# A new written order for every step of a post-norm attention and LoRA-expert block, with the pieces of x used as they land and the last two tiles normalised by VectorE

## The chip, the cores and the metric

The kernel runs on one core of one Trainium2 chip. The metric is the device time of one launch in microseconds (us). Three timed runs of the kernel before gave 686.65, 687.94 and 688.41 us, median 687.94. A difference of about 0.3% (2.06 us) is what a measurement of this kernel can tell from no change.

## The reference

All inputs are float32. `x` is (2, 512, 512): 1024 rows of width 512.

```python
q = (x @ Wq).reshape(B, S, 32, 128)          # 32 query heads of 128
k = (x @ Wk).reshape(B, S, 8, 128)           # 8 key/value heads
v = (x @ Wv).reshape(B, S, 8, 128)
scores = einsum(q, repeat(k, 4)) * 128 ** -0.5, causal mask
out = softmax(scores) @ repeat(v, 4)
x = layernorm(x + out @ Wo)                  # eps 1e-5, no scale or bias
base = x @ W_base.T + b_base
weights = sparsemax(x @ W_router.T + b_router)      # 8 experts
h = x @ lora_A                                      # 8 experts, rank 16
x = layernorm(x + base + (h * weights) @ lora_B)
```

## The kernel before

**Tiles.** A unit u (16 of them) is one key/value head g with its four query heads for one batch entry b: u = 2 g + b. It has four tiles of 128 query rows over the four heads, t = 4 u + i, 64 in all. Tile t attends to 128 (i + 1) keys and is scored in four pieces `("S", t, h)` whose width grows from 32 (i = 0, h = 0) to 512 (i = 3, h = 3) columns in steps of 32.

**Two halves of each number.** Nearly every operand is held as a high and a low float16 half, so that one product is three matmuls (high by high, high by low, low by high). ScalarE writes the high half, VectorE or GpSimd the low one. All operands are first scaled by a power of two that is derived from the largest absolute value: `("most", ...)` is the maximum on VectorE, `("bits", stage)` the exponent, `("turn", stage)` a matmul on TensorE that carries the row maxima across partitions, `("factor", stage)` the scale on VectorE. Until the first scales exist, K(0) and Q(0, 0..3) are computed from the raw float32 pieces of x and of the weights (the list `FIRST`), which is line 1062 (K) and line 1082 (Q).

**The steps of one tile.** `S` on TensorE (line 1113); the masked minimum on VectorE as the score leaves PSUM (line 937); `exp` on ScalarE (781); `inv`, the reciprocal of the sums, on VectorE (945); `norm`, the high half of the probabilities, on ScalarE (790), with zeros written by GpSimd (691); `rest`, the low half on VectorE (957) and then a DMA that transposes the probabilities (SyncE's queue, line 627), two for each tile, q = 0 and 1; `PV` on TensorE (1128); `O_hi` and `O_lo`, the two halves of the product (797, 963); `W`, the output projection (1138); and its sum with x on VectorE (974).

**What sets the order.** Each engine runs its instructions in the order of one written list of steps: `FIRST_STEPS` up to tile 5, `NEXT_STEPS` for 16 tiles, run three times with shifted numbers (tiles 6 to 53), and `LAST_STEPS`. Every engine walks over the same list and issues the part that is its own, so that the list sets the order on all five engines and on SyncE's DMA queue. The steps that empty a PSUM bank are put in by `evicted`. Three banks rotate among S, turn, zt, R and ht, five among the others; a step takes the bank that was given back first in the list.

**The second half of the block.** For each of eight row tiles k: `st1`, `ln1` (statistics and first layer norm), `zt` (transpose on TensorE), `R` (router and LoRA A in one product), `sp` (the sparsemax, seven short instructions on VectorE after one copy of half the product by ScalarE, line 809), `base` (line 1170), `ht` (transpose of the weighted h, 1187), `F` (LoRA B, 1193), `st2` (statistics from PSUM on VectorE, 1035 and 1037; variance, power and, for tiles that ScalarE normalises, the product `nmr` on GpSimd, 706, 708 and 712), and `fin` (the second layer norm: ScalarE, line 820, for tiles 0 to 6; VectorE, line 1029, for tile 7), with its output DMA.

**Loads.** The first loads go over two queues: ScalarE issues x(0, 1), x(0, 3), wq(0, 1) and wq(0, 3), and SyncE all others, wk(0), x(0, 0), x(0, 2), wq(0, 0), wq(0, 2) first.

## Time and profile before

| | us |
|---|---|
| timed runs | 686.65, 687.94, 688.41 |
| median | 687.94 |
| the profiled execution, its own time | 687.11 |
| its span, first to last instruction | 685.3 |
| TensorE busy | 664.1 |
| VectorE busy | 540.3 |
| ScalarE busy | 413.8 |
| GpSimd busy | 278.9 |
| mean granted TensorE clock | 0.993 of full |

The span is the time from the first to the last instruction; the profiled execution's own time is 1.8 us longer. PE is TensorE's matmuls, PEld its weight loads, DVE VectorE, ACT ScalarE, POOL GpSimd, and SPq, ACTq and POOLq the sequencers that issue DMAs and wait. TensorE is busy for all but 21 us of the span, so what matters in this profile is where those 21 us lie and what ended each gap.

### The profile page before, as it was taken

Reading aid. Unit: us, or ns where it says so; the run is one execution under the profiler, and the core shown is the slowest. Engines: PE = TensorE matmul, PEld = TensorE weight load, DVE = VectorE, ACT = ScalarE, POOL = GpSimd, SP = SyncE. Lnnn points to the kernel's source line nnn. Section 1 sums busy time; section 2 is a strip of 40 time slices with the busy share of each in tenths; the row PEclk is TensorE's granted clock in tenths of the full one; section 3 lists DMA queues with packets and bytes.
Section 4 is the critical chain, followed back from the end, with each engine's and each line's share of the span. In section 5 each row is a group of like instructions: output and inputs, shape, how many; then the busy total and the mean of one; then the engine's idle time right before and its main releaser. Section 6 shows DMA issues by size and latency. Waiting matters only on the chain.

```text
span 685.3 us, 11621 instructions
## 1 busy us (share of the span) xinstructions
PE 664.1 (97%) x3606; PEld 355.5 (52%) x3606; DVE 540.3 (79%) x1704; ACT 413.8 (60%) x1072; POOL 278.9 (41%) x424
## 2 busy tenths in 40 slices
PE   6799999999999999999999999999999999999996
PEld 3365545445555555455554555454555545456675
DVE  4898879876897679876897679877887676799774
ACT  1667666666647665667557665667556664776232
POOL 1676962157105562158005661258005550152132
PEclk9899999999999999999999999999999999999999
DMA  9456367352924257343924277343824335464311
GB/s 291 126 134 160 60 118 170 64 90 55 238 54 93 48 122 170 63 86 74 230 48 88 46 133 161 63 84 79 204 46 82 58 67 109 89 128 78 77 48 61
DMA packets 200782, 71.82 MB, mean 105 GB/s; under 512 B 169744, under 2 KB 192784, under 8 KB 200720
## 3 DMA queue, kind: packets, MB, share of 16 engines
q1 hardware_dynamic: 199376, 70.04, 47.3%
q10 hardware_dynamic: 1344, 1.05, 0.6%
q8 instruction: 28, 0.46, 0.3%
q14 instruction: 34, 0.28, 0.1%
HBM read 27.02 MB, written 2.10 MB: 42 GB/s over the span
## 4 chain that ended last, share of the span: by engine, by line
PE 75%; POOL 7%; DMA 7%; DVE 5%; SPq 2%; ACT 2%; issue 2%; POOLq 0%; DVEq 0%; ACTq 0%
PE bank L1138 19%; PE bank L1089 16%; PE bank L1128 12%; PE bank L1113 10%; DMA pT<-p 6%; PE bank L1101 5%; POOL raw L678 3%; PE bank L1170 3%; PE bank L1069 3%; PE bank L1082 2%; DVE p L957 2%; SPq L627 2%; POOL wo_odd L681 2%; PE bank L1072 2%; PE bank L1181 1%
## 5 line engine op out<-in xcount | busy, mean ns | idle before, releaser
L678 POOL TENSOR_SCALAR raw<-raw,scale_of 128x512 f32<-128x512 f32 x76 | 120.2, 1581 | 161.9 <-ACT wk L740 65.4
L781 ACT ACTIVATE pr<-pr,mx 128x96 f32<-128x96 f32 (+15 forms) x256 | 131.4, 513 | 81.7 <-DVE mx L937 81.5
L957 DVE SCALAR_TENSOR_TENSOR p<-pr,ri,p 128x256 f16<-128x256 f32 (+15 forms) x256 | 137.2, 580 | 36.3 <-ACT p L790 36.2
L1089 PE MATMUL bank<-xT,wq 128*128 128x512 f16 x720 | 164.4, 379 | 0.0
L790 ACT ACTIVATE p<-pr,ri 128x32 f16<-128x32 f32 (+15 forms) x256 | 118.6, 512 | 72.2 <-DVE ri L948 54.9
L937 DVE CUSTOM_DVE_ANT_0 pr<-bank,mask,back_of 128x32 f32<-128x32 f32 (+15 forms) x256 | 124.0, 493 | 47.1 <-PE bank L1113 46.9
L1113 PE MATMUL bank<-kT,qT 128*128 128x32 f16 (+15 forms) x768 | 125.7, 281 | 4.3 <-DVE qT L843 1.9
L1128 PE MATMUL bank<-pT,v 128*128 128x512 f16 x480 | 123.3, 379 | 3.5 <-DMA pT<-p 3.3
L1089 PEld LDWEIGHTS bank<-xT,wq 128*128 128x128 f16 x720 | 70.5, 98 | 81.7
L1113 PEld LDWEIGHTS bank<-kT,qT 128*128 128x128 f16 x768 | 67.6, 98 | 64.1 <-issue 3.5
L691 POOL MEMSET p<- 128x64 f16 (+2 forms) x192 | 34.0, 204 | 163.3 <-DMA pT<-p 163.3
L1138 PE MATMUL bank<-wo_odd,oT 128*128 128x512 f16 x384 | 97.7, 379 | 0.0
L1138 PE MATMUL bank<-wo_even,oT 128*128 128x512 f16 x384 | 95.7, 379 | 0.2 <-DVE oT L963 0.2
L1128 PEld LDWEIGHTS bank<-pT,v 128*128 128x128 f16 x480 | 45.2, 98 | 48.8 <-issue 6.7
L1138 PEld LDWEIGHTS bank<-wo_even,oT 128*128 128x128 f16 x384 | 36.1, 98 | 35.3 <-issue 0.4
L1138 PEld LDWEIGHTS bank<-wo_odd,oT 128*128 128x128 f16 x384 | 36.0, 98 | 34.4 <-issue 1.2
L963 DVE SCALAR_TENSOR_TENSOR oT<-bank,oT 128x512 f16<-128x512 f32 x64 | 43.8, 685 | 12.6 <-ACT oT L797 12.6
L797 ACT ACTIVATE oT<-bank 128x512 f16<-128x512 f32 x64 | 37.5, 585 | 26.1 <-PE bank L1138 14.5
L1101 PE MATMUL bank<-wv,xT 128*128 128x256 f16 x384 | 48.4, 277 | 1.4 <-DVE wv L833 1.4
L781 ACT ACTIVATION_READ_ACCUMULATOR pr<-pr,mx 128x1 f32 x256 | 48.1, 188 | 0.0
L974 DVE SCALAR_TENSOR_TENSOR y<-bank,back_of,y 128x512 f32<-128x512 f32 x64 | 47.2, 742 | 0.6 <-PE bank L1138 0.6
L863 DVE TENSOR_REDUCE rowmax<-raw 128x1 f32<-128x2048 f32 (+2 forms) x28 | 46.7, 1669 | 0.7 <-DMA raw<-in_wq 0.7
(121 smaller groups left out, 731.3 us busy)
## 6 DMA issues: line engine op xcount, KB each, us to landing
raw<-in_wo SPq DMA_DIRECT2D x32, 256.0 KB, 3.7
raw<-in_wq SPq DMA_DIRECT2D x30, 256.0 KB, 3.9
raw<-in_wk SPq DMA_DIRECT2D x8, 256.0 KB, 3.1
raw<-in_wv SPq DMA_DIRECT2D x8, 256.0 KB, 4.4
y<-in_x SPq DMA_DIRECT2D x1, 2048.0 KB, 12.7
pT<-p SPq DMA_TRANSPOSE x128, 3.7
out<-y SPq DMA_DIRECT2D x8, 256.0 KB, 2.0
pT<-in_xT SPq DMA_DIRECT2D x6, 256.0 KB, 7.8
```

Of the source, the lines that this page charges most:

```text
L678: eng.tensor_scalar(raw_of(name, key), raw_of(name, key), scale[0], None, ALU.mult).then_inc(sems["scaled"], 1)
L781: eng.activation(pr[:, t % 2, h, 0:w], pr[:, t % 2, h, 0:w], ACT.Exp, bias=mx[:, k:k + 1], scale=-1.0, accum_out=rs[:, k:k + 1]).then_inc( ...
L790: eng.activation(halves_of_probs(t, h)[0], pr[:, t % 2, h, 0:group(t, h)[1]], ACT.Copy, scale=ri[:, 1, k:k + 1]).then_inc(sems["p_hi"], 1)
L863: eng.tensor_reduce(out=to, in_=most_input(*key), axis=mybir.AxisListType.X, op=ALU.max, apply_absolute_value=True).then_inc(sems["most"], 1)
L937: eng.tensor_tensor_reduce(out=pr[:, t % 2, h, 0:w], in0=psum("S", t, h)[:, 0:w], in1=mask[:, 0:w], scale=score_scale(t), scalar=BIG, op0= ...
L957: made = eng.scalar_tensor_tensor(out=lo, in0=pr[:, t % 2, h, 0:group(t, h)[1]], scalar=ri[:, 1, k:k + 1], in1=hi, op0=ALU.mult, op1=ALU.s ...
L974: eng.scalar_tensor_tensor(out=y[:, k, :], in0=psum("W", t)[:, :], scalar=back_of[:, g, 2 + b:3 + b], in1=y[:, k, :], op0=ALU.mult, op1=AL ...
L1089: made = eng.matmul(out, wq[:, g % 2, w, h, c * 128:(c + 1) * 128], xT[:, x, c, b * 512:(b + 1) * 512], start=c == 0 and w + x == 0, stop= ...
L1101: made = eng.matmul(out, xT[:, x, c, at:at + 128], wv[:, w, c * 256:(c + 1) * 256], start=c == 0 and w + x == 0, stop=c == C - 1 and x == 1)
L1113: made = eng.matmul(out, qT[:, u % 2, q, at, :, :].rearrange("p h n -> p (h n)"), kT[:, u % 2, k, 32 * at:512], start=q + k == 0, stop=q == 1)
L1128: made = eng.matmul(out, v16[:, a, s, cols], turned_of(t, j, p).rearrange('p a m (h n) -> p a m h n', n=32), start=j == 0 and a + p == 0, ...
L1138: made = eng.matmul(psum("W", t)[:, :], oT[:, t % 2, a, h * 128:(h + 1) * 128], wo[g % 2][:, w, h, :], start=h == 0 and a + w == 0, stop=h ...
```

## The change

All three tables of steps are written anew. Every step of before is still there once, and none is added. The instructions of each engine are the same in kind and number, but for the ones named below; their order is new. `NEXT_STEPS` now begins a little elsewhere, so that the rule on which shifted steps exist became the function `there_is`. K(0) adds its four raw pieces of x in the order 1, 3, 0, 2 in place of 0, 1, 2, 3. The low halves of x(0, 2) and x(1, 3) move from GpSimd to VectorE, and those of x(0, 1) and x(1, 2) from VectorE to GpSimd. The second layer norm of tile 6 moves from ScalarE to VectorE, and GpSimd's `nmr` for it goes.

```diff
+def there_is(step):
+    name, *key = step
+    if name == "fetch":
+        return there_is(key)
+    if name == "wv":
+        return key[0] < G // 2
+    if name == "most":
+        return key[0] != "v" or key[1] < G // 2
+    return name not in ("wq", "wk", "wo") or key[0] < G
...
+X_LANDS = (1, 3, 0, 2)
...
-ON_DVE = [("wq", 0, 0), ("wq", 0, 1), ("wv", 0, 0), ("wv", 0, 1), ("x", 0, 1), ("x", 0, 3), ("x", 1, 1), ("x", 1, 2)]
+ON_DVE = [("wq", 0, 0), ("wq", 0, 1), ("wv", 0, 0), ("wv", 0, 1), ("x", 0, 2), ("x", 0, 3), ("x", 1, 1), ("x", 1, 3)]
...
-                    if k < 7:
+                    if k < 6:
                         pool.wait_ge(*done("st2", k))
                         eng.tensor_scalar(nmr[:, n:n + 1], mv[:, 4 + n, 0:1], -1.0, rstd[:, 4 + n:5 + n], ALU.mult,
...
-                elif name == "fin" and key[0] < 7:
+                elif name == "fin" and key[0] < 6:
...
-                elif name == "fin" and key[0] == 7:
-                    dve.wait_ge(*done("st2", 7))
-                    eng.tensor_scalar(y[:, 7, :], psum("base", 7)[:, :], mv[:, 7, 0:1], rstd[:, 7:8], ALU.subtract,
+                elif name == "fin" and key[0] > 5:
+                    k, = key
+                    n = k % 4
+                    dve.wait_ge(*done("st2", k))
+                    eng.tensor_scalar(y[:, k, :], psum("base", k)[:, :], mv[:, 4 + n, 0:1], rstd[:, 4 + n:5 + n], ALU.subtract,
...
-                        for c in range(C):
+                        for n, c in enumerate(X_LANDS):
                             pe.wait_ge(*fetched("x", b, c))
-                            made = eng.matmul(out, raw_of("wk", (0,))[:, c * 128:(c + 1) * 128], raw_of("x", (b, c)), start=c == 0, stop=c == C - 1)
+                            made = eng.matmul(out, raw_of("wk", (0,))[:, c * 128:(c + 1) * 128], raw_of("x", (b, c)), start=n == 0, stop=n == C - 1)
```

Of the tables, the head of `FIRST_STEPS`:

```diff
-    ("fetch", "wo", 0, 3), ("most", "x", 0, 1), ("table",), ("most", "x", 0, 0), ("warm", 2), ("consts",), ("most", "k", 0), ("most", "q", 0),
+    ("fetch", "wo", 0, 3), ("most", "k", 0), ("consts",), ("table",), ("most", "x", 0, 1), ("most", "x", 0, 0), ("most", "x", 0, 2), ("warm", 2),
```

VectorE's rows in the head, after the scales of x and of the first weights. Line 863 (879 after) with `pT` is the maximum of the second batch entry's x, line 833 (849) the low halves of x and wq, 838 (854) that of K(0), 843 (859) those of Q(0, h). Before:

```order
18 L926 TENSOR_SCALAR back_of<-xpower,power 128x1
19 L833 SCALAR_TENSOR_TENSOR xT<-pT,scale_of,xT 128x512
20 L863 TENSOR_REDUCE rowmax<-pT 128x1
21 L833 SCALAR_TENSOR_TENSOR xT<-pT,scale_of,xT 128x512
22 L877 TENSOR_SCALAR bound<-rowmax 128x1 x2
23 L881 TENSOR_SCALAR rowpower<-bound 128x1 x2
24 L838 SCALAR_TENSOR_TENSOR kT<-bank,first_scale,kT 128x512
25 L833 SCALAR_TENSOR_TENSOR wq<-raw,scale_of,wq 128x512
26 L843 SCALAR_TENSOR_TENSOR qT<-bank,first_scale,qT 128x16x32 x4
```

And in the changed kernel:

```order
18 L942 TENSOR_SCALAR back_of<-xpower,power 128x1
19 L879 TENSOR_REDUCE rowmax<-pT 128x1
20 L849 SCALAR_TENSOR_TENSOR xT<-pT,scale_of,xT 128x512 x2
21 L849 SCALAR_TENSOR_TENSOR wq<-raw,scale_of,wq 128x512
22 L893 TENSOR_SCALAR bound<-rowmax 128x1 x2
23 L897 TENSOR_SCALAR rowpower<-bound 128x1 x2
24 L854 SCALAR_TENSOR_TENSOR kT<-bank,first_scale,kT 128x512
25 L859 SCALAR_TENSOR_TENSOR qT<-bank,first_scale,qT 128x16x32 x4
```

The maximum over x(1) moved ahead of both low halves of x, and the low half of wq ahead of the exponent steps.

TensorE's rows around the first PV of tile 23, in the second pass through `NEXT_STEPS`: line 1089 (1107) is Q(7, 0), 1101 (1119) a product for V, 1113 (1131) the pieces S(25, 0) and S(25, 1), 1128 (1146) PV, 1150 (1168) the turn for the scales of unit pair 4. Before:

```order
267 L1089 MATMUL bank<-xT,wq 128x512 x12
268 L1101 MATMUL bank<-wv,xT 128x256 x12
269 L1113 MATMUL bank<-kT,qT 128x160 x3
270 L1128 MATMUL bank<-pT,v 128x4x4x32 x3
271 L1150 MATMUL bank<-ident,rowpower 128x128 x2
272 L1113 MATMUL bank<-kT,qT 128x192 x3
273 L1128 MATMUL bank<-pT,v 128x4x4x32 x9
```

And in the changed kernel:

```order
261 L1107 MATMUL bank<-xT,wq 128x512 x12
262 L1146 MATMUL bank<-pT,v 128x4x4x32 x3
263 L1131 MATMUL bank<-kT,qT 128x160 x3
264 L1119 MATMUL bank<-wv,xT 128x256 x12
265 L1168 MATMUL bank<-ident,rowpower 128x128 x2
266 L1131 MATMUL bank<-kT,qT 128x192 x3
267 L1146 MATMUL bank<-pT,v 128x4x4x32 x12
```

Row 270 of before is PV(23, 0), which stood ahead of the turn and of S(25, 1). After, it is the first of the twelve matmuls of row 267, behind both; row 262 is the last piece of PV(22), which stood earlier before.

ScalarE's last rows: line 809 (825) is the copy that opens a sparsemax, 815 (831) the high half of the weighted h, 820 (836) a layer norm `fin`. Before:

```order
794 L815 ACTIVATE hwT_hi<-bank 128x128 x2
795 L809 ACTIVATE rl<-bank 128x136
796 L815 ACTIVATE hwT_hi<-bank 128x128
797 L820 ACTIVATE y<-bank,nmr,rstd 128x512 x3
798 L272 UNCONDITIONAL_BRANCH
```

And in the changed kernel:

```order
793 L831 ACTIVATE hwT_hi<-bank 128x128
794 L836 ACTIVATE y<-bank,nmr,rstd 128x512
795 L825 ACTIVATE rl<-bank 128x136
796 L831 ACTIVATE hwT_hi<-bank 128x128
797 L836 ACTIVATE y<-bank,nmr,rstd 128x512
798 L288 UNCONDITIONAL_BRANCH
```

The layer norm of tile 4 moved from the end to a place between the high half for tile 6 and the copy that opens tile 7's sparsemax; that of tile 6 is gone from ScalarE.

## Rows read from the trace of the kernel before

**Rows 1.** The page, part 1: busy time, share, instructions

```profile
PE 664.1 (97%) x3606; PEld 355.5 (52%) x3606; DVE 540.3 (79%) x1704; ACT 413.8 (60%) x1072; POOL 278.9 (41%) x424
```

**Rows 2.** Waits on PE, whole span: engine line <- releaser: total, times, longest

```profile
PE bank L1062 <- DMA pT<-in_xT: 3.4, 1, 3.4
PE bank L1128 <- DMA pT<-p: 3.3, 6, 0.9
...
PE bank L1113 <- DVE power L889: 0.8, 1, 0.8
```

**Rows 3.** Timeline, PE and DVE: start us, duration us, what; in brackets idle before

```profile
6.59 5.17 PE L1062 MATMUL bank<-pT,raw 128*128 128x512 f32 x8 [3.39 <-DMA pT<-in_xT]
...
7.82 1.81 DVE L863 TENSOR_REDUCE xmax<-pT 128x1 f32<-128x512 f32 x2 [7.82 <-DMA pT<-in_xT]
...
10.91 2.29 DVE L863 TENSOR_REDUCE rowmax<-raw 128x1 f32<-128x2048 f32 x1 [0.68 <-DMA raw<-in_wq]
...
15.20 10.52 PE L1082 MATMUL bank<-pT,raw 128*128 128x512 f32 x24
...
18.92 0.75 DVE L833 SCALAR_TENSOR_TENSOR xT<-pT,scale_of,xT 128x512 f16<-128x512 f32 x1 [1.37 <-ACT xT L740]
...
27.38 0.45 PE L1113 MATMUL bank<-kT,qT 128*128 128x32 f16 x9 [1.66 <-DVE qT L843]
...
32.83 2.72 PE L1101 MATMUL bank<-wv,xT 128*128 128x256 f16 x12 [1.44 <-DVE wv L833]
```

**Rows 4.** Windows: stretch, PE busy, granted clock, DMA share, GB/s

```profile
33.00:34.00 1.00, 1.00 (x6) 0.50 1.04 406
```

**Rows 5.** Timeline, end of the kernel

```profile
675.82 0.29 DVE L1017 TENSOR_TENSOR hw<-rl,sp 128x128 f32<-128x128 f32 x1
...
676.71 0.27 PE L1187 MATMUL bank<-ident,hw 128*128 128x128 f32 x1
...
679.78 0.78 ACT L820 ACTIVATE y<-bank,nmr,rstd 128x512 f32<-128x512 f32 x1 [1.82 <-POOL nmr L712]
...
680.80 0.26 POOL L712 TENSOR_SCALAR nmr<-mv,rstd 128x1 f32<-128x1 f32 x1
...
681.14 0.22 POOL L706 TENSOR_SCALAR vs<-mv 128x1 f32<-128x1 f32 x1
```

**Rows 6.** Timeline, and DMA issues (last number: us to landing), first microseconds

```profile
0.72 0.45 SPq L609 DMA_DIRECT2D raw<-in_wk  x1
...
raw<-in_wk SPq DMA_DIRECT2D x1, 256.0 KB, 4.3
```

**Rows 7.** POOL's timeline, and tile wv: durations in ns min/median/max, 25 to 40 us

```profile
30.36 1.15 POOL L681 TENSOR_TENSOR xT<-pT,xT 128x512 f16<-128x512 f32 x1
...
L833 DVE SCALAR_TENSOR_TENSOR wv<-raw,scale_of,wv x2: 737/1190/1643, 30.4 to 32.0; 128x512 f16<-128x512 f32 x2
```

**Rows 8.** Timeline around tile 18, and its second transpose's us to landing

```profile
205.81 2.75 PE L1089 MATMUL bank<-xT,wq 128*128 128x512 f16 x12
...
209.15 0.61 DVE L937 CUSTOM_DVE_ANT_0 pr<-bank,mask,back_of 128x384 f32<-128x384 f32 x1
...
214.62 1.50 SPq L627 DMA_TRANSPOSE pT<-p  x1
...
DMA to landing us min/median/max: 3.7/3.7/3.7
...
219.83 0.81 PE L1128 MATMUL bank<-pT,v 128*128 128x512 f16 x3
```

**Rows 9.** Timeline of PE: two of the six waits for a transpose

```profile
152.95 1.46 PE L1128 MATMUL bank<-pT,v 128*128 128x512 f16 x6 [0.71 <-DMA pT<-p]
...
422.79 0.81 PE L1128 MATMUL bank<-pT,v 128*128 128x512 f16 x3 [0.88 <-DMA pT<-p]
```

**Rows 10.** Timeline, tile 57's last transpose, and its us to landing

```profile
586.34 1.25 SPq L627 DMA_TRANSPOSE pT<-p  x1
...
DMA to landing us min/median/max: 3.0/3.0/3.0
```

More of the change, by code:

```diff
@@ L82, in plan @@
             step = later(step, n)
-            if step[-3:-1] != ("wv", G // 2) and step[:2] != ("wv", G // 2) and step != ("most", "v", G // 2):
+            if there_is(step):
                 yield step
@@ new lines @@
+    ("S", 2, 0), ("exp", 1, 1), ("S", 2, 1), ("x", 1, 1), ("Vp", 0, 2), ("wq", 0, 2), ("norm", 0, 1), ("rest", 0, 1), ("wq", 0, 3), ("most", "k", 1),
+    ("exp", 2, 1), ("fetch", "wq", 1, 1), ("fetch", "wq", 1, 2), ("inv", 1, 1), ("exp", 2, 0), ("S", 2, 2), ("inv", 1, 0), ("K", 1), ("turn", "D"),
+    ("fetch", "wq", 1, 3), ("wq", 0, 1), ("norm", 1, 1), ("factor", "D"), ("S", 2, 3), ("norm", 1, 0), ("rest", 1, 1), ("inv", 2, 0), ("Vp", 0, 1),
+    ("rest", 1, 0), ("exp", 2, 2), ("exp", 2, 3), ("wo", 0, 2), ("wo", 0, 3), ("S", 3, 0), ("inv", 2, 1), ("fetch", "wo", 1, 3), ("most", "q", 1),
[3 rows of a table added]
@@ new lines @@
+    ("rest", 9, 0), ("W", 6, 1), ("bits", ("ov", 2)), ("exp", 9, 3), ("inv", 9, 1), ("norm", 9, 1), ("S", 10, 0), ("S", 10, 1), ("exp", 10, 0),
+    ("K", 3), ("W", 6, 2), ("W", 7, 0), ("turn", ("ov", 2)), ("factor", ("ov", 2)), ("W", 7, 1), ("rest", 9, 1), ("PV", 8, 0), ("exp", 10, 1),
+    ("S", 10, 2), ("exp", 10, 2), ("W", 7, 2), ("S", 10, 3), ("exp", 10, 3), ("W", 6, 3), ("inv", 10, 0), ("norm", 10, 0), ("inv", 10, 1),
[7 rows of a table added]
+    ("exp", 13, 2), ("rest", 12, 1), ("inv", 13, 0), ("W", 10, 1), ("wo", 2, 0), ("PV", 11, 3), ("norm", 13, 0), ("S", 13, 3), ("exp", 13, 3),
@@ L631, in _ @@
                     k, = key
-                    sp_.wait_ge(*done("ln2_dve" if k == 7 else "ln2_act", k))
+                    sp_.wait_ge(*done("ln2_dve" if k > 5 else "ln2_act", k))
                     eng.dma_start(out_d[k * 128:(k + 1) * 128, :], y[:, k, :]).then_inc(sems["out"], 16)
```

73 lines of the change are left out of this document (28 added, 45 removed), and 131 rows, old and new, of tables (FIRST_STEPS, LAST_STEPS, NEXT_STEPS).

## The prediction, as it was written before the result

> **What bounds the kernel now.** I read the page's first part, then the waits on TensorE, then the timeline where a wait stands. TensorE is busy 664.1 of 685.3 us [rows 1]. No matmul is added or removed, so at the full clock this is the floor, and a new order can win only from the other 21.2 us or lose by making new gaps. The waits on TensorE [rows 2] are few: 3.4 us at the start until x lands, 3.3 us in six waits of PV for transposed probabilities, 0.8 us for a bank that a scale step holds. Behind the start, VectorE is the late engine: TensorE waits 1.66 us before the first scores and 1.44 us before the first product for V [rows 3], each time for a low half from VectorE. Between about 25.7 and 32.8 us TensorE has little to do, and its clock then stands at half, 0.50, the level of 1.2 GHz [rows 4]. At the end TensorE is done some six microseconds before the span is; what follows is VectorE's statistics and GpSimd's chain for the last tiles [rows 5].
>
> **The head.** K(0) begins at 6.59, when x(0, 0) lands, although wk, issued at 0.72 with 4.3 us to landing [rows 6], is there at 5.02 and x(0, 1) before it. With x(0, 1) first K(0) can begin at 5.05, 1.54 us sooner. The last piece in the new order, x(0, 2), lands at 7.82, where VectorE's first maximum begins [rows 3]; K's last quarter comes later than that, so no wait arises inside. K(0)'s 5.17 us then end at 10.2 in place of 11.76. Q(0, 0), about 3.5 us (a third of the 10.52 us of the other three [rows 3]), is done at 13.6. Now the turn that follows in TensorE's order becomes the bound: it needs exponents that VectorE computes behind the maximum of q, which cannot begin before q's last piece lands, at 10.91, and takes 2.29 us. Before, the maximum of x(0, 3) came behind that one; now it is ahead of it, in the idle time before 10.91, which brings the exponents about 0.6 us forward (a third of the 1.81 us for pieces of one and two widths), to 14.0. So TensorE idles 0.4 us, and the three Qs start at 14.2 rather than 15.20, and end 1.0 sooner. VectorE itself gains more: the maximum of x(1), 2.28 us, fills the idle 1.37 us before 18.92. But the first scores need the last Q, its high half and its low half, so that surplus ends in an idle VectorE: S(0, 0) moves 1.0 us, from 27.38 to 26.4.
>
> From there the same instructions run on VectorE up to the low halves of wv, with one exception: a reciprocal and its two scalings, about 0.35 us, now stand ahead of them. If these delay wv, the head keeps 0.65 us. The trace says that they need not: of the two low halves of wv one took 737 ns and the other 1643, and the long one began at 30.42, just behind a GpSimd subtraction of x that ran from 30.36 to 31.51 [rows 7]. It ended 0.55 us behind it, as if it had begun when that one ended. GpSimd's work follows the end of Q and moves 1.0 us as well; the reciprocal would then stand in time that VectorE loses anyway. I take 1.0 us for the head; the bounds are 0 (a wait of 1.0 us arises at wv or behind) and 1.54 (all of K's advance).
>
> The Trainium skill, SBUF — State Buffer, section "SBUF: two separate sides", calls the port pair that VectorE and GpSimd share an exclusive lock, held for a whole instruction, where one with two SBUF inputs on VectorE is locked out by a GpSimd operation that began first. The trace agrees at this place, 1643 against 737 ns. By that rule the head gives 1.0 us, without it 0.65.
>
> **The first tiles.** The wait of 0.8 us for `power` [rows 2] is for the scales of the second head group. The step moves ahead of a low half of tile 3 on VectorE, over a microsecond, and TensorE's waiting step comes one PV and one S (0.65 and 0.2 us) sooner. I take 0.4 us gained; bounds 0 and 0.8.
>
> **The middle.** PV(t) waits for a chain that begins at the last score piece S(t, 3). I compare TensorE's work ahead of each PV in both lists: 0.65 us for a PV or W piece, 1.3 for a Vp, 2.6 for a Q (205.81 to 208.4 [rows 8]), 0.04 per 32 columns of S. Of the six waits, PV(33) now comes 5 us later, PV(6) 2.2 and PV(54) 1.4 later; their waits of 0.42, 0.25 and 0.62 go. PV(23) and PV(39) come only 0.4 us later (the V product and S(25, 0) were ahead before; only the turn and S(25, 1) are new): of 0.43 and 0.88 some 0.4 each goes. PV(11)'s 0.71 [rows 9] stays, since neither S(11, 3) nor PV(11) moves against it. Sum 0.42 + 0.25 + 0.62 + 0.8 = 2.1 us gained.
>
> Against this, some chains get less time. S(16, 3) and S(18, 3) move 2.6 us later, while PV(16) moves 0.65 later and PV(18) 0.65 sooner, and both repeat in three passes. In tile 18 the second transpose is issued at 214.62 and lands 3.7 us later, 1.5 us before PV(18) at 219.83 [rows 8]. If the chain slides by all of 2.6 us, PV(18) waits 1.8 us. But S(18, 3) stands directly ahead of the Q at 205.81, and VectorE took it up only at 209.15, 3.2 us after it was done [rows 8], being busy with other work; the slide then goes into that lateness. I take 0 for both. PV(57) comes 1.95 us sooner, and its last transpose, issued at 586.34 and landing 3.0 us later [rows 10], was used at once: up to 1.9 us of new wait. The load of the router weights, issued just ahead of this chain before, is now behind it, so I take 1.0 us. For places that I do not see, 0.3 us. New waits: 1.3 us; bounds 0 and 9.7, worked out below.
>
> **The end.** GpSimd runs the chains of tiles 5, 6 and 7 one behind the other. Without `nmr` for tile 6 the chain of tile 7 begins at 680.80 rather than 681.14 [rows 5]: 0.34 us. VectorE's layer norm of tile 6, 0.8 us, fits between the two powers and ends before tile 7's is due. The cost is on ScalarE: the layer norm of tile 4, 0.78 us, now stands ahead of the copy that opens tile 7's sparsemax. VectorE finished that at 676.11, and TensorE used it at 676.71 [rows 5]: 0.6 us of cover, so about 0.1 us is lost (0.7 of delay, the two overlapping a little at their ends). Net 0.25 us gained; bounds 0.5 lost (nothing hides the norm and the last chains slide) and 0.34.
>
> **The sum.** Head 1.0, first tiles 0.4, middle 2.1, end 0.25, new waits 1.3: 3.75 - 1.3 = 2.45 us gained. The profiled execution took 687.11 us with a span of 685.3, so the same execution of the new kernel would take 684.7 and have a span of 682.9. The median of the runs is 0.8 above the profiled execution; part of it is chance, so I add 0.3 and forecast 685.0 us.
>
> **The rivals.**
> (a) The new order only moves its waits. The six waits of before were six unforeseen ones as well; transposes compete with loads for landing times, and a list written anew meets others. What speaks for it: worked out as for tile 18, from landing and start, 21 of the 62 PVs behind the first two have less than 1 us of reserve. Against: five of the six known ones get more time. Then only head and end count: 687.11 - 1.65 gives 685.5, and from the median 686.3 us.
> (b) Slower: the slides are real. Place: the second transposes of tiles 16, 18, 54 and 57 and their repeats. Price at the full slide: 1.8, 1.2 and 1.5 us for tiles 18, 34 and 50 (2.6 + 0.65, less the reserve of each), 1.1 for 16 and for 32, 1.9 for 57, 1.1 for 54: 9.7 us. Less 3.75, that is 6 us slower, 693.9. It decides once the chains slide by over four tenths of the price. Against it is VectorE's lateness of 3.2 us in tile 18.
> (c) The clock. TensorE at half clock from about 30.5 to 36.5 loses some 2.0 us: the first V product takes 2.72 us [rows 3] where later ones of the same kind take 1.5, and two score pieces behind it lose 0.75. If the new order of the head keeps the full clock, this comes back: 683.0. For it: nothing but the shift by a microsecond. Against: the idle stretch between the last Q and the first V product is as long as before.
>
> **How the numbers follow.** The forecast's case 0.52, (a) 0.28, (b) 0.08, (c) 0.12. The forecast's own range is 683.6 to 686.4. For 8 in 10 it must reach to (a) with its scatter and to (c): 682.6 to 688.0. A difference of 0.3%, 2.06 us, is what a measurement can tell, so faster is below 685.88. In the forecast's case that holds 8 times in 10 (0.42), in (c) always (0.12), in (a) 3 in 10 (0.08): faster 0.62. Slower, above 690.0: (b) 0.07. Within: 0.31.
>
> **What the profile after would show.** K(0)'s first matmul at about 5.1 us, the first scores at 26.4 and the first V product at 31.8 (if at 32.2, the reciprocal was not hidden). TensorE's waits for transposes 1 to 3 us in place of 3.3, with none at PV(33) and PV(6), and a new one at PV(57). The first V product again at half clock. The last GpSimd power 0.25 us sooner against TensorE's last matmul. If waits for VectorE or for transposes exceed 5 us in the middle, (a) or (b) holds; a wait of over a microsecond behind 35 us that follows a maximum or a low half would tell that the head's gain was given back.

## The result and the profile after

| | before | after |
|---|---|---|
| timed runs, us | 686.65 to 688.41, median 688.01 of 4 | 680.35, 680.03, 682.15, 680.67, median 680.51 |
| ratio, 95% interval | | 0.9899, 0.9877 to 0.992 |
| profiled execution, own time | 687.11 | 680.35 |
| its span | 685.3 | 678.5 |

The forecast was 685.0 us, with a range of 682.6 to 688.0. The kernel became faster by 7.5 us by the medians and by 6.8 us by the two profiled executions, where 2.45 were forecast. The time lies below the range.

The page of after, part 1, answers to [rows 1]. TensorE's busy time fell by 0.8 us with the same 3606 matmuls, its idle time from 21.2 to 15.2 us.

```profile
PE 663.3 (98%) x3606; PEld 355.7 (52%) x3606; DVE 533.3 (79%) x1705; ACT 412.1 (61%) x1071; POOL 277.0 (41%) x423
```

The waits on TensorE of after, for [rows 2] (engine, line, what released it: us in total, times, longest):

```profile
PE bank L1131 <- DVE qT L859: 1.9, 2, 1.7
PE bank L1080 <- DMA raw<-in_wk: 1.8, 1, 1.8
PE bank L1119 <- DVE wv L849: 1.3, 1, 1.3
PE bank L1131 <- DVE mx L953: 1.0, 2, 0.8
PE bank L1146 <- DMA pT<-p: 0.9, 2, 0.5
```

The waits for transposes are 0.9 us in two places in place of 3.3 in six, and the wait for `power` is gone. The timeline of the head, for [rows 3 and 4], and then its window 33 to 34 us (granted clock 0.50):

```profile
5.04 5.53 PE L1080 MATMUL bank<-pT,raw 128*128 128x512 f32 x8 [1.85 <-DMA raw<-in_wk]
...
14.25 10.52 PE L1100 MATMUL bank<-pT,raw 128*128 128x512 f32 x24
...
26.43 0.45 PE L1131 MATMUL bank<-kT,qT 128*128 128x32 f16 x9 [1.66 <-DVE qT L859]
...
31.88 4.81 PE L1119 MATMUL bank<-wv,xT 128*128 128x256 f16 x24 [1.26 <-DVE wv L849]
```

```profile
33.00:34.00 1.00, 1.00 (x7) 0.69 (x6) 1.00 (x2) 0.00 (x0) 0.92 (x2) 0.50 0.95 304
```

K(0) at 5.04, the Qs at 14.25, the scores at 26.43, the V product at 31.88: each within 0.1 us of the forecast, again at half clock. The end of after, for [rows 5], in the order TensorE's last matmul, ScalarE's only late layer norm, GpSimd's power for tile 6 and its first instruction for tile 7:

```profile
672.36 0.39 PE L1211 MATMUL bank<-lb,hwT_lo 128*128 128x512 f32 x1
```

```profile
673.46 0.78 ACT L836 ACTIVATE y<-bank,nmr,rstd 128x512 f32<-128x512 f32 x1 [2.49 <-POOL nmr L728]
```

```profile
673.80 0.57 POOL L724 TENSOR_TENSOR rstd<-vs,mhalf 128x1 f32<-128x1 f32 x1
674.35 0.22 POOL L722 TENSOR_SCALAR vs<-mv 128x1 f32<-128x1 f32 x1
```

TensorE's last matmul ends at 672.75, 5.75 us ahead of the span's end; before it was 679.05, 6.25 ahead.

**Where the time came from.** I added up the columns that TensorE's matmuls stream, in order of time, in both traces. The table says how much sooner after reaches the same sum, from place to place (times of before):

| place | forecast | measured |
|---|---|---|
| head, to 40 us | 1.0 | 0.95 |
| first tiles, 40 to 77 | 0.4 | 1.44 |
| waits that go, 77 to 612 | 2.1 | 5.0: PV(6) 0.39, PV(11) 0.88, PV(23) 0.60, PV(33) and near it 0.3, PV(39) 1.04, PV(54) 0.78, S(59, 1) 0.91, PV(59) 0.12 |
| new waits, 77 to 612 | -1.3 | -1.45: PV(15) 0.65, PV(47) 0.52, S(60, 0) 0.28 |
| second half, 613 to TensorE's end | 0 | 0.4 |
| behind TensorE's last matmul | 0.25 | 0.5 |
| sum | 2.45 | 6.84 |

**A wait costs more than its number.** The rows of PV(15) and of what follows it, in after's timeline (start and busy time first), show why the busy time fell too:

```profile
186.87 0.81 PE L1146 MATMUL bank<-pT,v 128*128 128x512 f16 x3 [0.49 <-DMA pT<-p]
187.52 0.37 PE L1131 MATMUL bank<-kT,qT 128*128 128x160 f16 x3
```

Three matmuls take 0.81 us, but the next row starts 0.65 us behind their start: 0.16 us of each run of matmuls is its drain, which the next one covers. In front of a wait nothing covers it, and the profile counts it as busy. So a wait costs what it lists and 0.16 us: 0.49 and 0.65 at PV(15), 0.88 and 1.04 at PV(39). The trace of before has 16 breaks of over 0.15 us on TensorE, that of after 10; six times 0.16 is 1.0 us, and the busy time fell by 0.8. The Trainium skill, TensorE: Matmul & The Clock Gate, section "Single matmul latency", gives 166 ns beyond the streaming of the columns for one bfloat16 matmul at full clock; the 0.16 measured here on float16 agrees.

### The profile page after: what moved, and what is told of

Its sections match the earlier page's. It is cut to its first block, busy times and chain, and to the rows that moved or that the text cites. A ratio compares the mean times of both kernels' runs of the same rounds, so it can differ in the third digit from the quotient of the medians.

```text
span 678.5 us, 11619 instructions
## 1 busy us (share of the span) xinstructions
PE 663.3 (98%) x3606; PEld 355.7 (52%) x3606; DVE 533.3 (79%) x1705; ACT 412.1 (61%) x1071; POOL 277.0 (41%) x423
## 4 chain that ended last, share of the span: by engine, by line
PE 92%; DMA 3%; DVE 2%; issue 1%; SPq 1%; ACT 0%; POOL 0%; DVEq 0%; ACTq 0%
PE bank L1156 23%; PE bank L1107 22%; PE bank L1146 15%; PE bank L1131 13%; PE bank L1119 6%; PE bank L1087 4%; PE bank L1188 3%; DMA pT<-p 2%; PE bank L1090 2%; PE bank L1100 2%; DMA raw<-in_wq 1%; PE bank L1199 1%; PE bank L1211 1%; DVE p L973 1%; PE bank L1176 1%
## 5 line engine op out<-in xcount | busy, mean ns | idle before, releaser
L797 ACT ACTIVATE pr<-pr,mx 128x224 f32<-128x224 f32 (+15 forms) x256 | 131.1, 513 | 53.6 <-DVE mx L953 52.4
L806 ACT ACTIVATE p<-pr,ri 128x448 f16<-128x448 f32 (+15 forms) x256 | 117.9, 512 | 60.4 <-DVE ri L964 45.5
L973 DVE SCALAR_TENSOR_TENSOR p<-pr,ri,p 128x256 f16<-128x256 f32 (+15 forms) x256 | 125.4, 533 | 24.5 <-ACT p L806 23.5
L1131 PE MATMUL bank<-kT,qT 128*128 128x32 f16 (+15 forms) x768 | 122.3, 280 | 3.0 <-DVE qT L859 1.9
L707 POOL MEMSET p<- 128x192 f16 (+2 forms) x192 | 33.8, 204 | 191.8 <-DMA pT<-p 191.7
L1156 PE MATMUL bank<-wo_odd,oT 128*128 128x512 f16 x384 | 95.5, 379 | 0.0
L784 ACT ACTIVATE qT<-bank 128x512 f16<-128x512 f32 x60 | 35.1, 587 | 31.8 <-PE bank L1107 31.7
## 6 DMA issues: line engine op xcount, KB each, us to landing
y<-in_x SPq DMA_DIRECT2D x1, 2048.0 KB, 11.1
```

What stands on the lines that cost most here:

```text
L797: eng.activation(pr[:, t % 2, h, 0:w], pr[:, t % 2, h, 0:w], ACT.Exp, bias=mx[:, k:k + 1], scale=-1.0, accum_out=rs[:, k:k + 1]).then_inc( ...
L806: eng.activation(halves_of_probs(t, h)[0], pr[:, t % 2, h, 0:group(t, h)[1]], ACT.Copy, scale=ri[:, 1, k:k + 1]).then_inc(sems["p_hi"], 1)
L973: made = eng.scalar_tensor_tensor(out=lo, in0=pr[:, t % 2, h, 0:group(t, h)[1]], scalar=ri[:, 1, k:k + 1], in1=hi, op0=ALU.mult, op1=ALU.s ...
L1131: made = eng.matmul(out, qT[:, u % 2, q, at, :, :].rearrange("p h n -> p (h n)"), kT[:, u % 2, k, 32 * at:512], start=q + k == 0, stop=q == 1)
L1156: made = eng.matmul(psum("W", t)[:, :], oT[:, t % 2, a, h * 128:(h + 1) * 128], wo[g % 2][:, w, h, :], start=h == 0 and a + w == 0, stop=h ...
```

## The experiments

Fourteen kernels, and the changed kernel twice more (changed_again, changed_third), each timed beside before on the same chip. The numbers under "before" differ because before was timed anew with each group. Where the text says "before with" or "changed kernel with", the tables and the code are that kernel's but for what is named.

### Which part brings what

```diff
 x_lands:        before, only  X_LANDS = (1, 3, 0, 2)
 first_new:      before, X_LANDS, ON_DVE and FIRST_STEPS of the changed kernel
 first_next_new: the same, and NEXT_STEPS of the changed kernel
 last_new:       before, LAST_STEPS and "fin" of the changed kernel
```

> Tables and code of before; only K(0) adds its four raw pieces of x in the order 1, 3, 0, 2. Theory 1 (behind K the exponents are the bound: VectorE takes the maximum of x(0, 3) behind the 2.29 us maximum of q, so they are ready only at about 14.6): K(0) begins at 5.05, the three Qs start at about 14.7 instead of 15.20, S(0, 0) at 26.9, 0.5 us gained. Theory 2 (only the landing of x counts): the Qs start at 14.2, 0.95 us gained, as in the changed kernel. Theory 3: no gain, because VectorE's order keeps the first scores at 27.4.

> The changed kernel's FIRST_STEPS with its X_LANDS and ON_DVE; NEXT_STEPS, LAST_STEPS and the layer norms at the end as before. Theory 1 (gains add up by place in the list): TensorE reaches the columns that it had at 76.7 us in before 2.35 us sooner (0.95 of the head, 1.44 of the first tiles), keeps this, and the profiled execution has about 2.3 us less: 684.8. Theory 2 (the next table gives it back, because its chains get no more time and loads land as late): under 1.2 us is left at the end.

> FIRST_STEPS and NEXT_STEPS of the changed kernel, LAST_STEPS and layer norms as before. Theory 1 (the gain of the middle lies in NEXT_STEPS): against the kernel with only FIRST_STEPS new another 2.8 us less, minus the 0.78 us of tile 54's wait if that belongs to LAST_STEPS: about 682.0 to 682.8. Waits for p's transpose at tiles 6, 11, 23, 33, 39 gone, new ones at 15 and 47 (0.49, 0.36). Theory 2 (the tables interact; S and PV of LAST_STEPS meet other landings): more than 1 us away from that.

> Only LAST_STEPS new, with the last two tiles normalised by VectorE; K(0), FIRST_STEPS and NEXT_STEPS as before. Theory 1 (additive by place): the waits at tile 54 (0.62), S(59, 1) (0.55) and tile 59 (0.12) go, each with about 0.16 us that TensorE needs to fill again, one of 0.21 before S(60, ...) comes; about 0.4 us from the second half's order and 0.5 us at the end: 2.2 us less, 684.9. Theory 2 (the end alone counts, the rest came from the earlier tables): 0.5 to 0.8 us less.

| kernel | median | before beside it | ratio, interval | span |
|---|---|---|---|---|
| x_lands | 686.57 | 687.49 | 0.9988, 0.9974 to 1.0001 | 684.7 |
| first_new | 684.14 | 687.49 | 0.9954, 0.9942 to 0.9967 | 682.6 |
| first_next_new | 681.92 | 687.49 | 0.9929, 0.9907 to 0.9951 | 680.2 |
| last_new | 685.60 | 687.49 | 0.9972, 0.9957 to 0.9988 | 684.7 |

x_lands: the scores start at 26.77, 0.61 sooner, the exponents being the bound (TensorE waits 0.26 us for them at 14.43), as theory 1 had it with 0.5; the other third of the head's microsecond is put down to VectorE's new order, which no run has alone. By its time x_lands can't be told from before. The medians add up by table: FIRST_STEPS brings 3.4 us, NEXT_STEPS 2.2 and LAST_STEPS 1.9, together 7.5. last_new's profiled execution is only 0.6 us shorter than before's, because it has a wait of 2.12 us near 64 us that before's does not have (see the first tiles below). In detail the tables do interact: with only the first one new, PV(11) in the old middle waits no more, and PV(7) and PV(59) do, so that waits for transposes are 4.1 us in seven places there.

### What makes a transpose late: GpSimd's subtraction, or too little work ahead of PV

The low half of p is VectorE's last step before the transpose. The second pair of low halves of tile 11 in before (VectorE, timeline), and GpSimd at that time:

```profile
144.54 2.02 DVE L957 SCALAR_TENSOR_TENSOR p<-pr,ri,p 128x480 f16<-128x480 f32 x2 [0.83 <-ACT p L790]
```

```profile
144.22 1.16 POOL L681 TENSOR_TENSOR wq<-raw,wq 128x512 f16<-128x512 f32 x1
```

In after the same pair, with no subtraction beside it:

```profile
141.88 1.38 DVE L973 SCALAR_TENSOR_TENSOR p<-pr,ri,p 128x480 f16<-128x480 f32 x2 [0.83 <-ACT p L806]
```

Over the whole trace, 36 low halves of p start in before while GpSimd runs a subtraction or another instruction with two tensor inputs. Each is longer than the shortest of its shape by what is then left of GpSimd's instruction, less 0.19 us: 1.09 left, 0.90 longer; 0.38 left, 0.19 longer; under 0.2 left, nothing. That is 18.4 us in all, 21 of them being over 0.3 us longer. In after 27 start so, but only nine are over 0.3 us longer, 7.1 us in all. Those that start during GpSimd's scaling, which has one tensor input, are 0.06 longer on average. The page's groups of low halves of before and of after:

```profile
L957 DVE SCALAR_TENSOR_TENSOR p<-pr,ri,p 128x256 f16<-128x256 f32 (+15 forms) x256 | 137.2, 580 | 36.3 <-ACT p L790 36.2
```

```profile
L973 DVE SCALAR_TENSOR_TENSOR p<-pr,ri,p 128x256 f16<-128x256 f32 (+15 forms) x256 | 125.4, 533 | 24.5 <-ACT p L806 23.5
```

```diff
 pool_off (before with, in NEXT_STEPS):
-    ("rest", 11, 0), ("wq", 2, 1), ... ("rest", 11, 1), ("Vp", 1, 2),
+    ("rest", 11, 0), ... ("rest", 11, 1), ("wq", 2, 1), ("Vp", 1, 2),
-    ("PV", 5, 1), ("S", 7, 1), ("exp", 7, 1), ("fetch", "wo", 2, 0), ("wo", 1, 2),
+    ("PV", 5, 1), ("wo", 1, 2), ("S", 7, 1), ("exp", 7, 1), ("fetch", "wo", 2, 0),
 pv_later (before with):
-    ("Q", 5, 1), ("PV", 17, 0), ... ("Q", 5, 2),
+    ("Q", 5, 1), ... ("Q", 5, 2), ("PV", 17, 0),
     and PV(6, 0) behind W(5, 0), PV(54, 0) behind W(52, 2)
 pool_back: the changed kernel with both steps of pool_off where before has them
```

> The kernel before with two steps of GpSimd moved, and nothing of TensorE's, in NEXT_STEPS and so in three passes: the scaling of wq(2, 1) from just behind rest(11, 0) to just behind rest(11, 1), and that of wo(1, 2) three places up, to just behind PV(5, 1). Theory 1 (a low half of the probabilities that VectorE begins while GpSimd subtracts is held up by 0.6 to 0.9 us, and this delays the transpose and PV): the two low halves of tiles 7, 23 and 39 take 2.7 us together in place of 3.5, those of 11, 27 and 43 2.7 in place of 3.4, and the waits of PV(11), PV(23) and PV(39) (0.71, 0.43, 0.88) go or shrink to under 0.2 each; with some 0.16 us at each for TensorE to fill again 1.5 to 2.5 us less than before. Theory 2 (only the amount of TensorE's work between S(t, 3) and PV(t) counts, and it is unchanged here): the three waits stay within 0.2 us, and the time is that of before.

> The kernel before with three first pieces of PV later in TensorE's order and nothing of any chain changed: PV(17, 0) behind Q(5, 2) (three passes), PV(6, 0) behind W(5, 0) (three passes), PV(54, 0) behind W(52, 2). Theory 2 (distance): the waits of PV(33) 0.42, PV(6) 0.25 and PV(54) 0.62 go, each with 0.16 us of refilling: 1.8 us less. Theory 1 alone (chains are late for other reasons, the later PV delays the chain behind it): under 0.8 us less, with new waits behind these PVs.

> The changed kernel with GpSimd's collisions put back: the scaling of wq(2, 1) behind rest(11, 0) and that of wo(1, 2) ahead of exp(7, 2), as before has them, in three passes. Theory 1 (a held-up low half costs only what the reserve of its PV does not cover): the low halves of tiles 7, 23, 39 and 11, 27, 43 take 0.7 to 0.8 us longer again in each tile, but with reserves of 1.3, 2.2, 0.7 and 1.3, 1.7, 1.7 us only PV(39) waits, 0.1 to 0.5 us: 0.1 to 0.6 us more. Theory 2 (the VectorE time itself is what counts): some 4.6 us of VectorE work more, and over 1.5 us more in all.

A step `wq` or `wo` holds ScalarE's high half and GpSimd's scaling and subtraction, so that pool_off moves ScalarE's part with GpSimd's.

pool_off: 685.42 against 687.43, ratio 0.9976 (0.9959 to 0.9993). Tile 23 in it, VectorE and GpSimd, and then the same in before:

```profile
258.30 1.30 DVE L976 SCALAR_TENSOR_TENSOR p<-pr,ri,p 128x416 f16<-128x416 f32 x2 [0.48 <-ACT p L809]
```

```profile
257.41 1.15 POOL L700 TENSOR_TENSOR wo_odd<-raw,wo_odd 128x512 f16<-128x512 f32 x1
```

```profile
258.12 2.15 DVE L957 SCALAR_TENSOR_TENSOR p<-pr,ri,p 128x416 f16<-128x416 f32 x2 [0.50 <-ACT p L790]
```

```profile
258.55 1.24 POOL L681 TENSOR_TENSOR wo_odd<-raw,wo_odd 128x512 f16<-128x512 f32 x1
```

2.15 became 1.30, with no matmul moved. PV(11) now waits 0.35 (0.71 before) and PV(39) 0.16 (0.88), but PV(23) 0.50 (0.43). There the low halves were done 0.6 us sooner behind S(23, 3), but the first transpose, with five loads still on their way (four in before), kept SyncE's queue for 4.9 us in place of 3.2, and the second stood behind it. Theory 1 holds in its kind and not in its size: the collision goes and the waits get shorter, 1.0 us in all in the trace where 1.5 to 2.5 were expected, and only that of PV(39) is under 0.2. The medians differ by 2.0, with an interval of 0.5 to 2.8. These waits differ from one execution to the next: PV(11), PV(23) and PV(39) together wait 2.0 us in before, 1.8 to 2.8 in five other kernels whose second table is before's at these places (x_lands, last_new, factor_up, pv_later, before_wo_later), and 1.0 in pool_off.

The collision alone does not decide over PV(11). first_new has before's second table; its second pair for tile 11:

```profile
142.54 2.02 DVE L975 SCALAR_TENSOR_TENSOR p<-pr,ri,p 128x480 f16<-128x480 f32 x2 [0.83 <-ACT p L808]
```

It is held up as in before, and yet PV(11) does not wait: the second transpose lands 4.7 us after its issue there, as in after, against 6.2 in before and 6.5 in pool_off. No load was on its way in any of the four; what makes this landing slow or fast is open.

pv_later: 686.17 against 687.43, ratio 0.9980 (0.9971 to 0.9989). TensorE around PV(33), in pv_later and then in before:

```profile
360.03 2.75 PE L1110 MATMUL bank<-xT,wq 128*128 128x512 f16 x12
362.62 1.26 PE L1134 MATMUL bank<-kT,qT 128*128 128x416 f16 x6
```

```profile
361.93 0.81 PE L1128 MATMUL bank<-pT,v 128*128 128x512 f16 x3 [0.42 <-DMA pT<-p]
```

The waits at PV(33) and PV(54) go, with 0.61 and 0.77 us (listed: 0.42 and 0.62), the one at PV(6) too. But PV(7) behind it, whose transpose had landed only 0.18 us ahead of it in before (between a landing and a PV that waited for it lie 0.14), then waits 0.63, and PV(59) 0.56. So 1.3 us of the expected 1.8 came by the medians. Theory 2 holds too: both the amount of work ahead and the length of the chain count.

pool_back: 681.14, beside it the changed kernel at 681.22 (changed_again). The low halves of tiles 7, 23 and 39 take 3.53 us again in place of 2.69, and no new wait is listed, TensorE losing 0.1 us at PV(39): with 0.7 to 2.2 us between landing and PV in after the collision costs next to nothing, as theory 1 said. At tile 11 it didn't come back, since in the new order the subtraction falls elsewhere.

### The first tiles

```diff
 factor_up (before with):
-    ("rest", 3, 1), ("factor", ("qk", 1)),
+    ("factor", ("qk", 1)), ("rest", 3, 1),
 factor_down (the changed kernel with):
-    ("norm", 3, 1), ("factor", ("qk", 1)), ("S", 4, 1), ... ("rest", 3, 1),
+    ("norm", 3, 1), ("S", 4, 1), ... ("rest", 3, 1), ("factor", ("qk", 1)),
```

> The kernel before with one step moved: factor of (qk, 1), the step that frees the bank with power, goes ahead of rest(3, 1) on VectorE, where it stood behind it. Theory 1 (VectorE executes in order, idles 1.04 us for the high half and then takes 1.38 us, and power stands behind both): the wait of 0.81 us before S(4, ...) goes whole, about 1.0 us less. Theory 2 (as in my prediction, where the step was credited with half): 0.4 us less, the rest of the wait is taken by another VectorE result a few instructions on.

> The changed kernel with factor of (qk, 1) moved back behind rest(3, 1) on VectorE, where before has it. Theory 1 (VectorE is the bound of the first 65 us, and this step behind a low half that waits is what made the 0.81 us wait): a wait of 0.6 to 1.0 us for power comes back before a score piece of tile 4, and 0.7 to 1.1 us more are taken, whether TensorE's clock was halved before or not. Theory 2 (the wait went because of the whole order, this step is without effect): no wait, no difference.

> The changed kernel as it is, timed beside the others. Theory 1 (its time does not hang on whether the clock is halved at 30 to 36 us, since VectorE sets the pace until 61 us): runs with a mean clock of 0.998 and of 0.994 differ by under 0.4 us, and the profiled execution gives 680.3 whichever of the two it shows. Theory 2 (the clock counts): executions at full clock are 1.5 to 2 us faster.

factor_up: 687.04 against 687.43, ratio 0.9998 (0.9987 to 1.0008); for the median the 1.0 us of theory 1 is excluded. But its profiled execution had no wait for `power` to lose: the granted clock was 1.00 at 33 us (0.50 in before), and TensorE waited 2.12 us before S(4, 0) for VectorE's qT. The same 2.12 us stands in last_new, pool_off and pv_later, all with before's first table. factor_down: 680.97 beside the changed kernel's 681.22, where 0.7 to 1.1 us more were expected; in its trace a wait for `power` of 0.33 us came back, 0.48 with its refilling, about what the prediction had given the step; here a wait of 0.6 to 1.0 was expected. changed_again itself: 681.22, ratio 0.9908 (0.9879 to 0.9937); its profiled execution took 679.46 where 680.3 was expected whatever the clock.

What TensorE waits for near 61 us shows in two executions with the same first table. VectorE's low halves of tile 2, GpSimd's subtraction, and TensorE at S(4, 0), first in changed_again:

```profile
52.97 0.97 DVE L973 SCALAR_TENSOR_TENSOR p<-pr,ri,p 128x288 f16<-128x288 f32 x2
...
54.50 1.11 DVE L973 SCALAR_TENSOR_TENSOR p<-pr,ri,p 128x352 f16<-128x352 f32 x2
```

```profile
55.47 1.16 POOL L697 TENSOR_TENSOR wo_even<-raw,wo_even 128x512 f16<-128x512 f32 x1
```

and in the kernel that is called mended below:

```profile
53.30 1.41 DVE L975 SCALAR_TENSOR_TENSOR p<-pr,ri,p 128x288 f16<-128x288 f32 x2
...
55.27 2.01 DVE L975 SCALAR_TENSOR_TENSOR p<-pr,ri,p 128x352 f16<-128x352 f32 x2
```

```profile
55.33 1.53 POOL L699 TENSOR_TENSOR wo_even<-raw,wo_even 128x512 f16<-128x512 f32 x1
```

```profile
61.13 0.32 PE L1133 MATMUL bank<-kT,qT 128*128 128x32 f16 x6 [1.53 <-DVE qT L861]
```

Ahead of them VectorE waits for a load of wq and goes on at 48.14 in changed_again and at 48.47 in mended; it came 0.3 us later to its low halves, and so they collided: 3.4 us in place of 2.1, and a wait of 1.53 us in place of 0.08. Of nine profiled executions with the changed first table (in factor_down but for one step) six have 2.08 to 2.25 us and a wait of 0.08, three (first_next_new, factor_down, mended) 3.41 or 3.42 us and a wait of 1.24 to 1.53; none lies between, and changed_third's own belongs to the six. The three that collided ran at a granted clock of 1.00 at 33 us, but three of the other six did so too.

```diff
 wo_later (the changed kernel with):
-    ("rest", 2, 0), ("wo", 0, 0), ("exp", 3, 0), ("S", 3, 2), ("wo", 0, 1), ("Q", 1, 0),
+    ("rest", 2, 0), ("exp", 3, 0), ("S", 3, 2), ("Q", 1, 0), ("wo", 0, 0), ("wo", 0, 1),
 before_wo_later (before with): wo(0, 0) behind rest(2, 1)
```

> The changed kernel with one thing moved: the scalings of wo(0, 0) and wo(0, 1) (ScalarE's high half, GpSimd's low half) go behind Q(1, 0), so that GpSimd's subtraction for wo(0, 0) starts about 1 us later, at 56.5, when VectorE's second low half of tile 2 is over. Theory 1 (that subtraction and rest(2, 1) start within 0.4 us of each other, and an order of arrival decides over 1.3 us): rest(2, 0) and rest(2, 1) take 2.1 us together in every execution in place of 2.1 or 3.4, no wait of over 1 us for VectorE's qT at 61 us, runs scatter by about 1.4 us less upwards, median 0.4 to 1.0 us less than the changed kernel's beside it. Theory 2 (something else makes that wait, a late load of wq for one): the wait of 1.2 to 1.5 us at 61 us is found as often as before, the median is the same within 0.3. A possible cost in both: W(0, 1) waits up to 0.5 us for wo(0, 1).

> The kernel before with the scaling of wo(0, 0) behind rest(2, 1). Theory 1 (VectorE is the bound from 36 to 64 us, and rest(2, 1) took 1.53 or 2.00 us in place of 1.1 because of GpSimd's subtraction): rest(2, 1) takes 1.1 us, what follows on VectorE comes 0.4 to 0.9 us sooner, and the median is 0.4 to 0.9 us less. Theory 2: no effect, since GpSimd's later subtraction meets the next low half.

> The changed kernel as it is, timed beside these three. Theory 1: in its profiled execution either the low halves of tile 2 take 2.1 us and TensorE waits 0.1 us at 61 us, or they take 3.4 us and it waits 1.2 to 1.5 us; nothing between. Theory 2: values between these.

wo_later 681.22 beside the changed kernel's 680.73 (ratios 0.9908, 0.9888 to 0.9928, and 0.9903, 0.9888 to 0.9917): no gain, and no less scatter, against the 0.4 to 1.0 us expected. Neither profiled execution collided, so that the wait was not there to be taken away; that moving the subtraction prevents it is not shown. before_wo_later: rest(2, 1) takes 1.11 us in place of 1.53, as expected, but TensorE waits 0.55 us at S(4, 0) and elsewhere, and the ratio is 0.9994 (0.9981 to 1.0007): a gain of VectorE's that nothing made use of, where 0.4 to 0.9 us were expected.

### The end, and what is left

```diff
 fin6_act:     the changed kernel with "fin" of tile 6 on ScalarE and its nmr on GpSimd, as before
 mended:       the changed kernel with
-    ("PV", 14, 1), ("PV", 15, 0), ... ("PV", 14, 2), ("Vp", 1, 5), ("PV", 15, 1),
+    ("PV", 14, 1), ... ("PV", 14, 2), ("Vp", 1, 5), ("PV", 15, 0), ("PV", 15, 1),
-    ("F", 5), ("ht", 7), ("base", 7, 3, 4), ("F", 6), ("F", 7), ("st2", 5),
+    ("F", 5), ("st2", 5), ("ht", 7), ("base", 7, 3, 4), ("F", 6), ("F", 7),
     and W(56, 2) ahead of S(60, 0)
 mended_twice: mended and wo_later, and PV(16, 0) behind W(14, 3)
```

> The changed kernel with the layer norm of tile 6 on ScalarE again, and GpSimd's nmr for it. Theory 1 (GpSimd's chain sets the end): tile 7's first GpSimd instruction comes 0.34 us later against TensorE's last matmul, and the time from TensorE's last matmul to the end of the span grows from 5.75 to about 6.1 us; 0.3 us more in all. Theory 2 (VectorE's two layer norms, which run one behind the other, set it): no difference.

> The changed kernel with three moves at the waits that it has left: PV(15, 0) behind Vp(1, 5) (three passes), W(56, 2) ahead of S(60, 0), and st2(5) ahead of ht(7). Theory (each wait costs its listed time and 0.16 us of refilling): PV(15) 0.49 and PV(47) 0.36 go, with 0.16 each, S(60, 0)'s 0.21 goes; at the end GpSimd's chain for tile 7 starts 0.3 to 0.4 us sooner against TensorE's last matmul: 1.6 to 1.9 us less than the changed kernel. Rival (the PVs of 15 and 47 are needed for oT soon after, so the wait moves): under 0.8 us less.

> The three moves of the first mended kernel, the later scaling of wo(0, 0) and wo(0, 1), and PV(16, 0) behind W(14, 3) (three passes), since it waited 0.89 us there. Theory (the terms add up): against the changed kernel PV(15) 0.65 and PV(47) 0.5 less, S(60, 0) 0.2, the end 0.38, the first tiles 0.4 to 1.0: 2.0 to 2.7 us less. Rival (an order written anew meets new waits of the same size elsewhere): under 1.2 us less.

fin6_act: 680.45 against 687.43 (0.9901, 0.9886 to 0.9916), which its time does not set apart from the changed kernel. In the trace, from TensorE's last matmul to the end of the span it takes 6.24 us in place of 5.75. GpSimd's chain in it:

```profile
673.53 0.57 POOL L726 TENSOR_TENSOR rstd<-vs,mhalf 128x1 f32<-128x1 f32 x1
674.20 0.26 POOL L730 TENSOR_SCALAR nmr<-mv,rstd 128x1 f32<-128x1 f32 x1
674.55 0.22 POOL L724 TENSOR_SCALAR vs<-mv 128x1 f32<-128x1 f32 x1
```

From the power (673.53) to tile 7's first instruction it is 1.02 us with nmr; in after, without, the two start at 673.80 and 674.35, 0.55 apart. The step was worth 0.47 us, and all of it reached the end.

mended: 678.86, beside it the changed kernel at 681.22; mended_twice: 678.43 against before's 687.66, ratio 0.9871 (0.9855 to 0.9886), the changed kernel beside it 680.73 (0.9903, 0.9888 to 0.9917). The waits on TensorE for transposes in mended_twice:

```profile
PE bank L1148 <- DMA pT<-p: 0.2, 1, 0.2
```

In mended the waits at 15 and 47 went and one of 0.89 came at PV(16), as its rival said. The move of W(56, 2) gained nothing: 0.21 us before S(60, 0) became 0.24 before S(60, 3). The time from TensorE's last matmul to the end fell from 5.75 to 5.4 us. mended's 2.4 us against the changed kernel are more than the 1.6 to 1.9 expected and not shown, since the intervals overlap (0.9845 to 0.9903 and 0.9879 to 0.9937). With PV(16) later too, in mended_twice, nothing came back. It is 2.3 us ahead of the changed kernel beside it, within the 2.0 to 2.7 expected; the intervals of the two ratios just miss each other. Of its expected terms the one for the first tiles is not seen in the trace.

## Why the prediction was wrong

**Right.** The head, at each point, with the reciprocal hidden. The low halves of wv in after (durations in ns, first and last start), and GpSimd's subtraction:

```profile
L849 DVE SCALAR_TENSOR_TENSOR wv<-raw,scale_of,wv x2: 736/934/1133, 30.0 to 31.0; 128x512 f16<-128x512 f32 x2
```

```profile
29.41 1.15 POOL L697 TENSOR_TENSOR xT<-pT,xT 128x512 f16<-128x512 f32 x1
```

The first one started during the subtraction, took 1133 ns and ended 0.55 us behind it, as in [rows 7]. The waits of PV(33) and PV(6) went for the reason given, more work of TensorE's ahead of them. That of PV(54) went by luck, as far as this reason goes. S(54, 3) moved later by more than PV(54), so that TensorE has 1.2 us less to do between the two. But the last transpose of tile 54 lands 4.4 us sooner behind S(54, 3). In before the low halves for its first transpose were done at 553.67, and SyncE issued it only at 557.83, as GpSimd finished writing the zeros among the probabilities:

```profile
557.40 0.49 POOL L691 MEMSET p<- 128x192 f16 x3
```

In after these zeros are written at 545.61, before S(54, 3) begins. S(18, 3)'s slide went into VectorE's lateness, as I had it: VectorE took it up 0.04 us after its end (3.2 before), its PV has 1.4 us of reserve (1.5 before). The size of the new waits, 1.3 for 1.45, is luck: none of it is at PV(57), where the chain became 3.1 us shorter, and all at places that I did not name.

**Wrong, the step that failed: the middle, "PV(11)'s 0.71 stays, since neither S(11, 3) nor PV(11) moves against it", and with it the halves given to PV(23) and PV(39).** It failed twice over.

First, the premise is false. In the old list W(8, 0) stands ahead of S(11, 3), in the new one behind it, and the other pieces between S(11, 3) and PV(11) are the same ones; so TensorE has one piece of 0.65 us more to do before PV(11). The rows of before, W(8, 0), S(11, 3) and W(8, 1):

```profile
139.49 0.81 PE L1138 MATMUL bank<-wo_odd,oT 128*128 128x512 f16 x3
140.14 0.81 PE L1113 MATMUL bank<-kT,qT 128*128 128x512 f16 x3
140.78 0.81 PE L1138 MATMUL bank<-wo_odd,oT 128*128 128x512 f16 x3
```

And of after, S(11, 3), a V product, W(8, 0) with W(8, 1), and PV(11):

```profile
136.75 0.81 PE L1131 MATMUL bank<-kT,qT 128*128 128x512 f16 x3
137.39 1.47 PE L1119 MATMUL bank<-wv,xT 128*128 128x256 f16 x12
138.70 1.46 PE L1156 MATMUL bank<-wo_odd,oT 128*128 128x512 f16 x6
...
149.33 1.46 PE L1146 MATMUL bank<-pT,v 128*128 128x512 f16 x6
```

From the end of S(11, 3) to PV(11) it is 11.8 us in after. In before it is 12.0, of which the wait and its drain are 0.9, so 11.1 of work. That is 0.64 us of the 0.88 gained there.

Second, the step took the length of the chain from S(t, 3) to the transposed p as given and compared only TensorE's work. The chain got shorter. At tile 11 it took 11.9 us from the end of S(11, 3) to the landing and takes 10.5. VectorE's maximum comes 0.7 us later and the low halves are 0.8 shorter, so that the second transpose is issued as late as before (5.8 us and 5.7); the gain is the landing, 4.7 us after the issue in place of 6.2. At tiles 23 and 39 the second low half begins 1.6 us sooner behind S(t, 3), 0.8 of it because the first is not held up. At tile 23 the new list also has three loads just ahead of the transposes where the old one has six. I had the cause of the 0.8 at hand, for I used it for wv in the head [rows 7], and did not ask where else VectorE's low halves meet GpSimd's subtractions: the pairs of 2.02 and 2.15 us stand in the trace of before beside ones of 1.38 and 1.30.

The worth: 0.88 at PV(11) for nothing in the sum, and 0.84 more than forecast at the other two. By TensorE's work PV(23) and PV(39) gained 0.36 each, as forecast; the shorter chain gave 0.24 at each of PV(11) and PV(23) and 0.68 at PV(39), 1.2 us in all. pool_off, which ends these collisions in before and moves no matmul, brings 1.0 us in its trace. It does not split the 1.2 us into collision, landing and loads, and how the landing at tile 11 got faster is open.

**Wrong, sizes.** S(59, 1)'s 0.55 was in no term and gave 0.91. The first tiles gave 1.44 for 0.4: the step `factor` is worth 0.5 in factor_down's trace, which also collided; that two waits of 0.19 and an earlier VectorE make the rest is my reading, no run shows it. PV(6) comes 2.8 us later behind S(6, 3), not 2.2. The end gave 0.5 for 0.25: nmr costs 0.47, not 0.34 (I took the distance of two starts and left out that nmr itself starts later than what follows it would), and ScalarE's layer norm of tile 4, for which 0.1 was taken off, cost nothing to be seen: TensorE has no break of over 0.07 us behind 600. And every wait was counted as listed, without the 0.16 us of draining: with six breaks fewer, 1.0 us.

**The rivals.** (a) and (b) did not come. (c), the full clock in the head, comes and goes in both kernels. Of 73 runs of before 32 had a mean granted clock of at least 0.997, with a median of 687.4, and 27 one of 0.993 to 0.996, with 687.1; so it is worth nothing there. (The other 14, below 0.993, have a median of 688.6; in the changed kernel four such runs have 682.0. What differs in these no trace shows.) The traces say why it is worth nothing. When the granted clock is 1.00 at 33 us, K(0) takes 6.1 to 6.6 us in place of 5.2 to 5.7, so that the scores start later. And in before VectorE is at work for 39.9 of the 44 us from 26 to 70, and for 41.5 in an execution at full clock (pool_off's), where the low halves of tile 2 collide and TensorE waits 2.12 us for VectorE. In the changed kernel, where they often don't collide, changed_again kept 1.28 us of it behind 61 us against after. Of 14 runs the four with at least 0.997 have a median of 680.0, the six with 0.993 to 0.995 one of 680.6, which is too few to call it a gain.
